# A layer's attention operands stacked with seven transfers instead of thirteen, and a new order ahead of a selective scan

## The chip, the cores and the metric

The kernel runs on one core of one Trainium2 chip. The metric is the device time of one execution, in microseconds (us). The kernel is one hand-written program: each engine (PE for matmuls, DVE, ACT, POOL, and SP, which only issues DMAs) has its own list of instructions, and semaphores order the lists against each other.

## The reference

Two layers act on x, 1024 tokens of 512 numbers. Each layer modulates a layer norm with six vectors that come from silu(c) @ wmod, and adds its two branches under gates whose magnitude is at least 0.25.

```python
ga = (2 * (ga >= 0) - 1) * jnp.maximum(jnp.abs(ga), 0.25)
h = _layernorm(x, axis=-1) * (1 + ca) + sa
x = x + ga * _L0_attn_ref(h, ...)
...
# layer 0, "attention": a selective scan
xp = jnp.einsum('bld,rd->blr', x, x_proj_w)            # 16 dt columns, 16 B, 16 C
dt = jax.nn.softplus(jnp.einsum('blr,dr->bld', dt_in, dt_proj_w) + dt_proj_b)
h = dA_t * h + dBx_t                                   # 512 channels x 16 states
y = jnp.einsum('bdn,bn->bd', h, C_t)
...
# layer 0, ffn: base linear + 8 LoRA experts under a router (softmax over 15, top 8)
...
# layer 1: 32 heads of 16, causal, linear position bias (ALiBi)
scores = jnp.einsum('bqhd,bkhd->bhqk', q, k) * SCALE + bias
out = jnp.einsum('bhqk,bkhd->bqhd', jax.nn.softmax(scores), v)
...
# layer 1, ffn: silu(gate) * up, truncated, down, truncated
```

## The kernel before

Everything stays in on-chip memory but for one round trip through DRAM, described below. Channels or tokens lie on the 128 partitions; T = 1024 tokens are two halves of 512, and 512 channels are four chunks (DC) of 128.

**Ahead of the scan.** DVE normalises the four token tiles of the first half, sums wmod weighted by silu(c) into two vectors, and PE turns them into columns (L757). PE transposes the tiles (L747), ACT applies scale and shift (L517), PE projects to dt, B and C (`x_proj`, L771; `dt_proj`, L775). ACT and DVE then work out softplus for each chunk by a longer formula: on ACT an absolute value (L542), Exp, "+1" (L545), Square, Ln (L548); on DVE the argument with the bias `dtb` (L1222) and corrections (L1234 to L1249). B and C, rows of `BCs`, are spread over the partitions by PE for each state (`broadcast`, L841 and L849). Then the second half is projected, `y_start` (L855) puts D * h into the four accumulating banks, and the scan begins.

**The scan** runs over N_ALL = 32 steps m (2 halves x 16 states), each over 4 chunks: DVE forms dBx (L1266) and scans (L1288), ACT makes the decay (L636), POOL multiplies with C (L468), PE accumulates (L889). `SLOTS` names small PE jobs that are put between steps, among them the other modulation columns (`cols`). In step 4 DVE works out the first gate in four small operations (L1293 to L1296). The ffn of layer 0 follows; its `router` (L902) takes 16 matmuls of a half after all four chunks of the transposed input.

**Queries and keys of layer 1** are 16 blocks of 128 columns x 512 tokens, in the order `QK_ORDER` (L1019, one block is four fp32 matmuls, which the trace records as eight). ACT evacuates a block to `qkf` (2 buffers), DVE splits it into three bf16 parts in `qkp` (3 buffers: block i waits until the write of block i - 3 has landed), and SP writes the parts to the DRAM array `parts_dram` [part, row, token] (L372). A row of it is a head's dimension.

**Stacks.** For each of 8 groups g of 4 heads `load_stack(g)` reads the parts back into one of three `stack` buffers: 96 partitions are six bands of 16 (a head's 16 dimensions), which hold the parts of q in the order (0,0,1,1,0,2) and those of k in the order (0,1,0,1,2,0), so that one matmul with 120 rows gives the product in full precision; 24 more rows hold the position bias (`alibi`). It takes twelve transfers of 16 partitions x 4 heads x 2 KB and one for alibi. A stack's semaphore `stk` counts all of them, and PE waits for it before the group's first scores (L963). All of these transfers and the writes are issued by SP, in one list.

**Order.** `S_QK` is the number of the QK block behind which the first early scores stand; `s_early(i)` says how many units of scores PE and DVE do behind block i. DVE's list has the split of block i, and then the maxima of those units. A unit's PSUM bank (ring of three) comes free when DVE has taken its maximum (L1403, L1407). The V projection (L1036) follows the 16 blocks, with more scores between. Stack g goes to buffer g % 3, and its load is issued when the group three before it is done with its buffer.

Of the kernel before, what the change touches and what calls it, by code (L numbers as in the profile page):

```python
# [32 lines left out]
S_QK = 8  # L33
# [9 lines left out]
PARTS_Q = (0, 0, 1, 1, 0, 2)  # L43
PARTS_K = (0, 1, 0, 1, 2, 0)
# [48 lines left out]
def program(nc, a, out):  # L93
    ctx = ExitStack()
    with ctx:
# [36 lines left out]
        dtb = tiny("dtb", [P, DC])  # L132
# [17 lines left out]
        dtw = at("dtw", G_AT + 8, [RANK, D], off=2304 + 2048 + 1024)  # L150
# [15 lines left out]
        dtin = at("dtin", 30, [RANK, HALF])  # L166
# [61 lines left out]
        for n in ("in_c in_x0 in_x1 in_wb in_w1 in_id in_misc in_l0 in_lf in_attn in_proj in_gate in_up in_down wd_p0 wd_p1 wd_p2 wd_r0 wd_r1 in_att "  # L228
                  "c_exp c_silu mod_acc mod_mm mod_ev mod_ga negA setup "
                  "ln_ve ln_rstd ln_norm ln_tr ln_hT "  # L230
                  "xp_mm xp_in bc_part bc_sub xp_bc dt_mm sp_a sp_rd sp_e sp_w sp_ln sp_z sp_u sp_w1 sp_g sp_cl sp_pu dg "
# [59 lines left out]
        for i_ in range(6):  # L291
            SLOTS[1 + i_] = ("cols", 0, 2 + i_ // 2, i_ % 2 * 2)
# [9 lines left out]
        MM_L0, MM_ALL, EV_ALL = 9, 1 + len(MODS), 2 + len(MODS)  # L302
# [10 lines left out]
        def _(sp):  # L313
# [11 lines left out]
            misc = [(sel[:].bitcast(U16), a["sel"]), (nA[:], a["A_log"]), (dtb[:], a["dt_b"]), (Dp[:], a["D"]),  # L325
# [85 lines left out]
        def _(pool):  # L411
# [7 lines left out]
            pool.memset(ones[:], 1.0).then_inc(S["setup"], 1)  # L419
            link(pool.memset(mhalf[:], -0.5))  # L420
# [77 lines left out]
        def _(act):  # L498
# [22 lines left out]
            act.wait_ge(S["in_misc"], 16 * 6)  # L521
# [16 lines left out]

            def soft(c):
                src = ps[:, 4 + c, :]  # L540
                act.wait_ge(S["dt_mm"], c + 1)
                A_(sp_log[:, c, :], src, ACT.Abs, bias=dtb[:, c:c + 1]).then_inc(S["sp_a"], 1)  # L542
                act.wait_ge(S["sp_a"], c + 1)
                link(A_(sp_exp[:, c, :], sp_log[:, c, :], ACT.Exp, scale=-1.0))
                A_(sp_w[:, c, :], sp_exp[:, c, :], ACT.Copy, bias=1.0).then_inc(S["sp_w"], 1)  # L545
# [4 lines left out]
            for part in range(3):  # L550
                bc_part(0, part)
            for c in range(DC - 1):
                soft(c)
            ln_out(0, 0, 0, 1, (1,))
            soft(DC - 1)

            def z_out(c):
                act.wait_ge(S["dt_mm"], DC + (c if c else DC))
                A_(dtT[:, c, half(1)], ps[:, c, :], ACT.Identity, bias=dtb[:, c:c + 1]).then_inc(S["sp_z"], 1)

            act.wait_ge(S["xp_mm"], 2)
            act.wait_ge(S["dt_mm"], DC)
            A_(dtin[:], ps[0:RANK, 0, :], ACT.Copy).then_inc(S["xp_in"], 1)
            bc_part(1, 0)
            z_out(1)
            bc_part(1, 1)
            z_out(2)
            bc_part(1, 2)
            act.wait_ge(S["negA"], 2)

            def prepare(i):
                c, step = i // 7, i % 7
                z, lg, e, w = dtT[:, c, half(1)], sp_log[:, c, :], sp_exp[:, c, :], sp_w[:, c, :]
                if step == 0:
                    act.wait_ge(S["sp_z"], c + 1)
# [19 lines left out]
            def slot_out(m):  # L595
# [5 lines left out]
                act.wait_ge(S["mod_mm"], 2 + MOD_NO[m])  # L601
# [20 lines left out]
            def keep_state(i):  # L622
                m, c = i // DC, i % DC
# [116 lines left out]
        def _(pe):  # L740
# [90 lines left out]
            def broadcast(m):  # L831
# [11 lines left out]
                if m:  # L843
                    pe.wait_ge(S["c_evac"], m)
# [760 lines left out]
```

## Time and profile before

| what | value |
|---|---|
| median of 3 runs | 940.39 us (939.13 to 942.77) |
| the profiled execution's own time | 939.05 us |
| its span in the trace | 937.2 us |
| PE busy | 855.5 us (91%) |
| DVE busy | 762.1 us (81%) |
| ACT busy | 439.2 us (47%) |
| POOL busy | 262.6 us (28%) |
| PE's wait for the first stack | 8.3 us |

The span is the time between the first and the last instruction in the trace; the execution's own time is 1.85 us longer. Busy shares are averages over stages with different limits, so each stage is read by itself.

### The profile page before, as it was taken

What the parts mean: (1) busy time and instruction counts of PE and PEld (TensorE: products, weight loads), DVE (VectorE), ACT (ScalarE), POOL (GpSimd) and SP (SyncE); (2) the same over time, 40 slices, a digit from 0 to 9 for tenths busy, and PEclk for the clock granted to TensorE, in tenths of its full rate; (3) what the DMA queues carried; (4) which work ended last, traced back from release to release, by engine and by line L of the source; (5) the groups of instructions that cost most, each with busy time, mean ns of one, the idle gap of its engine ahead of it and who ended that gap; (6) DMA issues with size and microseconds to landing.
All of it is one profiled execution on the core that took longest, in us unless ns stands there. A gap on an engine that the chain in (4) does not pass through costs nothing.

```text
span 937.2 us, 12092 instructions
## 1 busy us (share of the span) xinstructions
PE 855.5 (91%) x4165; PEld 410.1 (44%) x4165; DVE 762.1 (81%) x1624; ACT 439.2 (47%) x828; POOL 262.6 (28%) x213
## 2 busy tenths in 40 slices
PE   3787978899978998799999999999999999999996
PEld 2334524454427453344444444444434444444442
DVE  6589999999996876598899989998245799776776
ACT  2667655656652031100666666667541656433100
POOL 1047899999994000031000000000001334000000
PEclk8689799999999999899999999999999999999999
DMA  9200060300006006820552255310015000000001
GB/s 347 94 1 0 1 269 1 134 1 1 0 1 201 0 29 151 197 69 1 87 78 47 34 77 78 53 29 1 2 39 202 1 0 0 1 0 1 12 34 46
DMA packets 27238, 54.34 MB, mean 58 GB/s; under 512 B 5876, under 2 KB 12660, under 8 KB 25896
## 3 DMA queue, kind: packets, MB, share of 16 engines
q1 hardware_dynamic: 27176, 53.56, 21.7%
q8 instruction: 33, 0.54, 0.3%
q14 instruction: 29, 0.24, 0.1%
HBM read 44.96 MB, written 8.39 MB: 57 GB/s over the span
## 4 chain that ended last, share of the span: by engine, by line
PE 62%; DVE 6%; DMA 1%; POOL 1%; SPq 1%; ACT 1%; issue 0%; POOLq 0%
PE ps L1135 16%; PE ps L997 7%; PE ps L1146 6%; PE ps L979 6%; PE ps L1019 5%; PE ps L963 4%; PE ps L966 3%; PE ps L1056 3%; PE ps L908 3%; PE ps L1036 3%; PE ps L982 2%; DVE ps L1403 1%; PE ps L747 1%; PE ps L902 1%; DMA stack<-in_alibi 1%; PE ps L911 1%
## 5 line engine op out<-in xcount | busy, mean ns | idle before, releaser
L700 ACT ACTIVATE prob<-ps 128x512 f32<-128x512 f32 x288 | 160.1, 599 | 124.4 <-PE ps L982 96.2
L468 POOL TENSOR_TENSOR hC<-hs,C_sb 128x512 f32<-128x512 f32 x128 | 162.1, 1283 | 59.3 <-DVE hs L1288 51.3
L889 PE MATMUL ps<-hC,identf 128*128 128x512 f32 x256 | 136.1, 634 | 24.1 <-POOL hC L468 22.9
L979 PE MATMUL ps<-stack 123*128 123x512 bf16 (+3 forms) x384 | 113.8, 327 | 0.2
L636 ACT ACTIVATE ps<-dtT,nA 128x512 f32<-128x512 f32 x128 | 88.2, 689 | 47.5 <-DVE hs L1288 47.5
L424 POOL TENSOR_TENSOR rstd<-veps,mhalf 128x4 f32<-128x4 f32 x8 | 8.1, 1012 | 358.4 <-DVE veps L1173 358.4
L1410 DVE TENSOR_REDUCE mrow<-ps 128x1 f32<-128x512 f32 x128 | 82.0, 683 | 11.4 <-PE ps L966 11.2
L889 PEld LDWEIGHTS ps<-hC,identf 128*128 128x128 f32 x256 | 44.0, 194 | 90.0 <-POOL hC L468 77.3
L997 PE MATMUL ps<-prob,V 128*32 128x512 f32 (+3 forms) x768 | 81.6, 498 | 0.7 <-ACT prob L700 0.7
L1135 PE MATMUL ps<-hT,wg 128*128 128x512 f32 (+1 forms) x176 | 79.1, 592 | 0.0
L1135 PE MATMUL ps<-hT,wu 128*128 128x512 f32 (+1 forms) x176 | 79.1, 592 | 0.0
L1288 DVE TENSOR_TENSOR_SCAN hs<-ps,dBx 128x512 f32<-128x512 f32 x64 | 77.6, 1212 | 0.6 <-ACT ps L636 0.5
L1266 DVE TENSOR_TENSOR dBx<-uT,ps 128x512 f32<-128x512 f32 x112 | 73.8, 660 | 5.1 <-PE ps L841 3.9
L1403 DVE CUSTOM_DVE_ANT_0 ps<-ps,negT 128x128 f32<-128x128 f32 x256 | 66.2, 322 | 12.1 <-PE ps L963 11.3
L963 PE MATMUL ps<-stack 120*128 120x128 bf16 x640 | 62.1, 221 | 13.5 <-DMA stack<-in_alibi 8.3
L963 PEld LDWEIGHTS ps<-stack 120*128 120x128 bf16 x640 | 42.6, 98 | 62.8 <-DVE mrow L1407 13.8
L1288 DVE TENSOR_TENSOR_SCAN hs<-ps,state,dBx 128x512 f32<-128x512 f32 x56 | 69.9, 1269 | 0.2 <-ACT ps L636 0.2
L1407 DVE TENSOR_REDUCE mrow<-ps 128x4 f32<-128x512 f32 x96 | 62.5, 684 | 2.3 <-PE ps L963 1.5
L1019 PE MATMUL ps<-hT,wattn 128*128 128x512 f32 x128 | 58.2, 607 | 0.0
L1146 PE MATMUL ps<-wdp,inter 128*128 128x512 bf16 (+1 forms) x264 | 57.2, 379 | 0.0
L1135 PEld LDWEIGHTS ps<-hT,wu 128*128 128x128 f32 (+1 forms) x176 | 33.0, 188 | 42.5 <-issue 42.5
L966 PE MATMUL ps<-stack 120*128 120x512 bf16 x128 | 48.8, 383 | 2.9 <-DVE V L1388 2.1
(194 smaller groups left out, 1334.1 us busy)
## 6 DMA issues: line engine op xcount, KB each, us to landing
stack<-parts_dram SPq DMA_DIRECT2D x96, 128.0 KB
wmod<-in_wmod SPq DMA_DIRECT2D x4, 1536.0 KB, 11.3
parts_dram<-qkp SPq DMA_DIRECT2D x16, 384.0 KB, 2.7
wmod<-in_wmod SPq DMA_DIRECT2D x4, 1024.0 KB, 9.8
wattn<-in_wattn SPq DMA_DIRECT2D x1, 3072.0 KB, 10.0
wg<-in_wg SPq DMA_DIRECT2D x1, 2752.0 KB, 12.3
wu<-in_wu SPq DMA_DIRECT2D x1, 2752.0 KB, 10.5
wd<-in_wd SPq DMA_DIRECT2D x1, 2560.0 KB, 11.4
```

The lines of the kernel that those rows point to most:

```text
L468: pool.tensor_tensor(hC[:, c, :], hs[:, c, :], C_sb[:, m % 2, :], ALU.mult).then_inc(S["hc_done"], 1)
L636: A_(ps[:, DA_BANK + c % 2, :], dtT[:, c, half(h)], ACT.Exp, scale=nA[:, c * NS + s:c * NS + s + 1]).then_inc(S["da_done"], 1)
L700: A_(prob[:, u % 4, j, :], ps[:, 3 + F % 3, :], ACT.Exp).then_inc(S["exp_done"], 1)
L889: mm(ps[:, c, :], identf[:], hC[:, c, :], start=False, stop=(s == NS - 1), skip_group_check=True).then_inc(S["sum_done"], 1)
L963: ins = mm(ps[:, bank, tile(j_)], qk[0:ATT_S, 0, j_, tile(i)], qk[0:ATT_S, 1, j_, tile(kb)], start=True, stop=True)
L979: ins = mm(ps[:, bank, col:col + w], qk[0:ATT_ALL, 1, j, tile(kb)], qk[0:ATT_ALL, 0, j, q0:q0 + w], start=True, stop=not diag)
L997: ins = mm(ps[32 * j:32 * j + 32, 6 + b, q0 % HALF:q0 % HALF + w], V[:, kb, g * GH + j, :], prob[:, U % 4, j, col:col + w], start=(kb == 0 ...
L1019: ins = mm(ps[:, qk_bank(i), :], wattn[:, k, ob * P:(ob + 1) * P], hT[:, k, half(h)], start=(k == 0), stop=(k == DC - 1))
L1135: ins = mm(ps[0:M, 2 * s + b, :], w[:, k, ib * P:ib * P + M], hT[:, k, half(h)], start=(k == 0), stop=(k == DC - 1))
L1146: ins = mm(ps[:, 4 + t % 4, :], inter[0:M, k, tile(t)], wdp[0:M, part, k, :], start=(k == 0 and part == 0), stop=(k == IC - 1 and part == 2))
L1288: v.tensor_tensor_scan(hs[:, c, :], ps[:, DA_BANK + c % 2, :], dBx[:, c, :] if c < mine else dB3[m % 2], init, ALU.mult, ALU.add).then_inc ...
L1410: v.reduce_max(mrow[:, 0, j, i:i + 1], ps[:, bank, :], AX).then_inc(S["m_done"], 1)
```

## The change

**Stacks.** The host permutes the columns of w_attn and b_attn so that within a group's 64 rows the dimension runs outside and the head inside. The four heads' rows of one dimension are then contiguous in `parts_dram` (8 KB), and a band of 16 partitions takes one run per partition. Parts (0,1,2), (0,1) and (0) of q go to bands 0 to 2, 3 to 4 and 5 with one transfer each, and so do those of k, where one part is read three times, twice and once. With alibi that is seven transfers. The first stack is loaded behind write 4 instead of 5, the second behind write 6 instead of 7, and `S_QK` is 9 instead of 8.

**Ahead of the scan.** The bias of dt is a 17th row of `dtw` against a row of ones in `dtin`, so its DMA and L1222 go; the argument is read from PSUM where it is used. ACT normalises tiles 1 to 3 of the first half. "+1" moves from ACT to DVE (`plus`). The columns of the first gate (16 matmuls, one ACT copy, four DVE operations) move from the scan to a place ahead of it. `broadcast` is split into B and C, B of step 0 stands before the second projection, both of step 1 stand before `y_start`, and `y_start` is interleaved with the sums of step 0. The scan's states are kept for two chunks at a time. The router waits for each chunk of its first tile by itself.

```diff
-S_QK = 8
+S_QK = 9
...
             def load_stack(g):
-                for o, order in ((0, PARTS_Q), (1, PARTS_K)):
-                    for b, part in enumerate(order):
-                        at_ = o * D + g * GH * HD
-                        load(stack[g % 3][16 * b:16 * b + 16, o, :, :],
-                             parts_dram[part, at_:at_ + GH * HD, :].rearrange("(h d) t -> d h t", d=HD), stk[g % 3])
-                load(stack[g % 3][ATT_K:ATT_S, 1, :, :].bitcast(U16),
-                     a["alibi"][g * GH:(g + 1) * GH, :, :].rearrange("h r t -> r h t"), stk[g % 3])
+                for first, count in ((0, 3), (3, 2), (5, 1)):
+                    at_ = g * GH * HD
+                    q = parts_dram[0:count, at_:at_ + GH * HD, :].rearrange("q (d h) t -> q d (h t)", h=GH)
+                    load(stack[g % 3][16 * first:16 * (first + count), 0, :, :], q, stk[g % 3])
+                    at_, part = D + g * GH * HD, 3 - count
+                    k = parts_dram[part:part + 1, at_:at_ + GH * HD, :].rearrange("q (d h) t -> q d (h t)", h=GH)                         .to_broadcast([count, HD, GH * T])
+                    load(stack[g % 3][16 * first:16 * (first + count), 1, :, :], k, stk[g % 3])
+                load(stack[g % 3][ATT_K:ATT_S, 1, :, :].bitcast(U16), a["alibi"][g], stk[g % 3])
...
-                if i == 5:
+                if i == 4:
...
-                if i == 7:
+                if i == 6:
                     load_stack(1)
...
+            for t in range(1, 4):
+                A_(xn0[:, t, :], x_tok[:, t, :], ACT.Identity, bias=nmean[:, t:t + 1]).then_inc(S["cent"], 1)
...
+                A_(xn0[:, t, :], xn0[:, t, :], ACT.Copy, scale=rstd[:, t:t + 1]).then_inc(S["ln_norm"], 1)
...
-                A_(sp_w[:, c, :], sp_exp[:, c, :], ACT.Copy, bias=1.0).then_inc(S["sp_w"], 1)
...
+            for c in range(DC):
+                for kk in range(DC):
+                    ins = mm(ps[:, C_BANK, c:c + 1], wmod[:, kk, 2 * D + c * P:2 * D + (c + 1) * P], sc[:, 0, kk:kk + 1],
+                             start=(kk == 0), stop=(kk == DC - 1))
+            ins.then_inc(S["mod_mm"], 1)
+            broadcast_b(0)
             x_proj(1)
...
+            broadcast(1)
             pe.wait_ge(S["sp_z"], DC)
-            for c in range(DC):
-                y_start(0, c)
...
+                    if m == 0:
+                        y_start(0, c)
...
-                ts(dtT[:, c, half(0)], ps[:, 4 + c, :], dtb[:, c:c + 1], 0.0, ALU.add, ALU.max).then_inc(S["sp_rd"], 1)
...
+                ts(sp_w[:, c, :], sp_exp[:, c, :], 1.0, None, ALU.add).then_inc(S["sp_w"], 1)
...
+                stt(dt, ps[:, 4 + c, :], 0.0, lg, ALU.max, ALU.add).then_inc(S["sp_rd"], 1)
...
-                    if c == 2 and m == 4:
-                        v.wait_ge(S["mod_ev"], 4)
-                        link(ts(modt[:, 1, :], modc[:, 0, 2, :], 0.0, 2.0, ALU.is_ge, ALU.mult))
```

SP's list at the first two stacks, before (L372 writes a block's parts, L315 loads; a shape is that of the destination):

```order
L372 DMA parts_dram<-qkp 128x3x512 x6
L315 DMA stack_126<-parts_dram 16x4x1024 x12
L315 DMA stack_126<-in_alibi 24x4x1024
L372 DMA parts_dram<-qkp 128x3x512 x2
L315 DMA stack_127<-parts_dram 16x4x1024 x12
L315 DMA stack_127<-in_alibi 24x4x1024
L372 DMA parts_dram<-qkp 128x3x512 x8
```

and of the change:

```order
L371 DMA parts_dram<-qkp 128x3x512 x5
L313 DMA stack_126<-parts_dram 48x1x4096 x2
L313 DMA stack_126<-parts_dram 32x1x4096 x2
L313 DMA stack_126<-parts_dram 16x4096 x2
L313 DMA stack_126<-in_alibi 24x4096
L371 DMA parts_dram<-qkp 128x3x512 x2
L313 DMA stack_127<-parts_dram 48x1x4096 x2
L313 DMA stack_127<-parts_dram 32x1x4096 x2
L313 DMA stack_127<-parts_dram 16x4096 x2
L313 DMA stack_127<-in_alibi 24x4096
L371 DMA parts_dram<-qkp 128x3x512 x9
```

Each stack stands one write earlier, and nine writes instead of eight are behind the second.

PE's list at the first scores, before (L1019 QK blocks of four matmuls, L1025 the mask for DVE, L963 scores of stack 0):

```order
L1019 MATMUL ps<-hT,wattn 128x512 x28
L1025 MATMUL ps<-identb,negm 128x128
L963 MATMUL ps<-stack_126 128x128 x8
L1019 MATMUL ps<-hT,wattn 128x512 x4
L963 MATMUL ps<-stack_126 128x128 x4
L1019 MATMUL ps<-hT,wattn 128x512 x4
L963 MATMUL ps<-stack_126 128x128 x8
```

and of the change:

```order
L1064 MATMUL ps<-hT,wattn 128x512 x32
L1070 MATMUL ps<-identb,negm 128x128
L1008 MATMUL ps<-stack_126 128x128 x8
L1064 MATMUL ps<-hT,wattn 128x512 x4
L1008 MATMUL ps<-stack_126 128x128 x4
L1064 MATMUL ps<-hT,wattn 128x512 x4
L1008 MATMUL ps<-stack_126 128x128 x8
```

One QK block more stands ahead of the first scores; two blocks stand ahead of this piece in both.

PE's list at the start of the scan, before (L747 transposes, L771 the projection, L841 and L849 B and C, L775 and L782 the second half's dt and B/C parts, L855 `y_start`, L889 the sums):

```order
L747 MATMUL ps<-identf,xn_90 128x128 x16
L771 MATMUL ps<-hT,xpw 64x512 x4
L841 MATMUL ps<-BCs,sel 128x512
L849 MATMUL ps<-BCs,sel 128x512
...
L775 MATMUL ps<-dtin,dtw 128x512 x2
L855 MATMUL ps<-hT,dgD 128x512 x4
L841 MATMUL ps<-BCs,sel 128x512
L849 MATMUL ps<-BCs,sel 128x512
L889 MATMUL ps<-hC,identf 128x512 x4
```

and of the change:

```order
L771 MATMUL ps<-identf,xn_90 128x128 x16
L863 MATMUL ps<-sc,wmod 128x1 x16
L827 MATMUL ps<-BCs,sel 128x512
L795 MATMUL ps<-hT,xpw 64x512 x4
L840 MATMUL ps<-BCs,sel 128x512
...
L799 MATMUL ps<-dtin,dtw 128x512 x2
L827 MATMUL ps<-BCs,sel 128x512
L840 MATMUL ps<-BCs,sel 128x512
L898 MATMUL ps<-hT,dgD 128x512
L933 MATMUL ps<-hC,identf 128x512
L898 MATMUL ps<-hT,dgD 128x512
```

The gate's 16 matmuls and B of step 0 stand before the second projection, and B and C of step 1 before `y_start` instead of behind it.

## Rows read from the trace of the kernel before

**Rows 1.** The page's first line.

```profile
span 937.2 us, 12092 instructions
```

**Rows 2.** Windows: busy us (instructions) of PE, PEld, DVE, ACT, POOL; granted clock; DMA share; GB/s.

```profile
52.70:281.00 228.30, 197.08 (x649) 95.58 (x650) 222.28 (x251) 139.01 (x303) 199.91 (x160) 0.96 0.11 42
...
371.30:379.70 8.40, 0.08 (x2) 0.04 (x2) 2.44 (x5) 0.69 (x1) 0.00 (x0) 0.81 1.08 175
...
448.00:660.00 212.00, 206.19 (x1912) 99.39 (x1916) 187.70 (x659) 145.12 (x267) 0.00 (x0) 1.00 0.35 53
```

**Rows 3.** Timeline of PE around the first scores: start, length, work, [idle before, releaser].

```profile
379.66 1.04 PE L963 MATMUL ps<-stack 120*128 120x128 bf16 x8 [8.32 <-DMA stack<-in_alibi]
380.49 5.08 PE L1019 MATMUL ps<-hT,wattn 128*128 128x512 f32 x8
...
385.63 3.65 PE L1019 MATMUL ps<-hT,wattn 128*128 128x512 f32 x8
```

**Rows 4.** Timeline of SP, writes and stack loads, and the load issues of groups 2, 3.

```profile
360.68 0.36 SPq L372 DMA_DIRECT2D parts_dram<-qkp  x1
...
364.60 5.74 SPq L315 DMA_DIRECT2D stack<-parts_dram  x12
...
378.77 33.50 SPq L372 DMA_DIRECT2D parts_dram<-qkp  x8
...
448.95 6.69 SPq L315 DMA_DIRECT2D stack<-parts_dram  x12
...
477.70 6.65 SPq L315 DMA_DIRECT2D stack<-parts_dram  x12
```

**Rows 5.** The page's DMA issues: count, KB each, us to landing.

```profile
parts_dram<-qkp SPq DMA_DIRECT2D x16, 384.0 KB, 2.7
...
stack<-r SPq DMA_DIRECT2D x24, 8.0 KB, 1.9
```

**Rows 6.** DMA of the window in which stack 3 is loaded, 477.75 to 495.

```profile
DMA packets 1071, 1.81 MB, mean 105 GB/s; under 512 B 204, under 2 KB 204, under 8 KB 1068
```

**Rows 7.** Windows of 2 us: the first weights, behind PE's wait, stack 3's load.

```profile
6.00:8.00 2.00, 0.00 (x0) 0.00 (x0) 1.41 (x3) 0.00 (x0) 0.00 (x0) 1.00 1.04 422
...
380.00:382.00 2.00, 2.00 (x9) 1.27 (x8) 1.57 (x9) 0.00 (x0) 0.00 (x0) 0.50 1.11 278
...
483.00:485.00 2.00, 2.00 (x19) 1.01 (x12) 1.47 (x3) 1.29 (x4) 0.00 (x0) 1.00 1.10 134
```

**Rows 8.** DMA issues of the window 366 to 380 alone.

```profile
parts_dram<-qkp SPq DMA_DIRECT2D x3, 384.0 KB, 11.2
```

**Rows 9.** Timeline of PE: V begins, first scores of groups 2 and 3.

```profile
408.58 1.02 PE L1036 MATMUL ps<-wattn,hT 128*128 128x512 f32 x2
...
466.23 0.39 PE L963 MATMUL ps<-stack 120*128 120x128 bf16 x4
...
497.02 0.39 PE L963 MATMUL ps<-stack 120*128 120x128 bf16 x4
```

**Rows 10.** Timeline at the scan's start, all engines.

```profile
32.66 0.63 ACT L545 ACTIVATE sp_w<-sp_exp 128x512 f32<-128x512 f32 x1
33.19 0.61 ACT L546 ACTIVATE uT<-sp_exp 128x512 f32<-128x512 f32 x1
...
52.74 1.22 DVE L1288 TENSOR_TENSOR_SCAN hs<-ps,dBx 128x512 f32<-128x512 f32 x1
...
54.43 5.98 PE L855 MATMUL ps<-hT,dgD 128*128 128x512 f32 x8 [1.89 <-ACT dtT L559]
...
60.67 0.69 DVE L1266 TENSOR_TENSOR dBx<-uT,ps 128x512 f32<-128x512 f32 x1 [3.29 <-PE ps L841]
```

**Rows 11.** Timeline of DVE in step 4: the gate's four operations, first and last.

```profile
88.09 0.97 DVE L1293 TENSOR_SCALAR modt<-modc 128x4 f32<-128x4 f32 x1
...
90.52 0.16 DVE L1296 SCALAR_TENSOR_TENSOR modc<-modt 128x4 f32<-128x4 f32 x1
```

**Rows 12.** The chain that ended last, 281 to 300: the router's matmuls.

```profile
289.80 5.82 PE ps L902 x32
```

More of the change, by code:

```diff
@@ L290, in program @@
         SLOTS = {}
-        for i_ in range(6):
-            SLOTS[1 + i_] = ("cols", 0, 2 + i_ // 2, i_ % 2 * 2)
+        for i_ in range(4):
+            SLOTS[3 + i_] = ("cols", 0, 3 + i_ // 2, i_ % 2 * 2)
         for i_ in range(2):
@@ L548, in soft @@
                 A_(sp_log[:, c, :], sp_w[:, c, :], ACT.Ln).then_inc(S["sp_ln"], 1)
-            for part in range(3):
-                bc_part(0, part)
-            for c in range(DC - 1):
+            bc_part(0, 0)
+            magnitude(0)
+            bc_part(0, 1)
+            soft(0)
+            bc_part(0, 2)
+            for c in range(1, DC - 1):
+                magnitude(c)
                 soft(c)
             ln_out(0, 0, 0, 1, (1,))
+            magnitude(DC - 1)
+            act.wait_ge(S["mod_mm"], 2)
+            A_(modc[:, 0, 2, :], ps[:, C_BANK, 0:DC], ACT.Copy).then_inc(S["mod_ev"], 1)
             soft(DC - 1)
@@ L650, in _ @@
                 for c in range(DC):
-                    decay(m * DC + c)
+                    if m:
+                        decay(m * DC + c)
                     if m == 0 and c < 2:
@@ L783, in bc_rest, with slot_read, broadcast_b, broadcast_c @@
                     .then_inc(S["bc_sub"], 1)
+            def slot_read(m):
+                if m in SLOTS:
+                    if SLOTS[m][0] == "y":
+                        pe.wait_ge(S["x0"], SLOTS[m][3] + 1)
+                    else:
+                        pe.wait_ge(S["mod_ev"], 4 + MOD_NO[m])
+            def broadcast_b(m):
+                h, s = m // NS, m % NS
+                if s == 0:
+                    pe.wait_ge(S["xp_bc"], h + 1)
+                if m == 0:
+                    pe.wait_ge(S["sp_rd"], 2)
+                    pe.wait_ge(S["sp_a"], 2)
+                else:
+                    pe.wait_ge(S["dbx_done"], dbx_count(m - 1, DC - 1 if m <= NS else DC - 2))
+                    if m > NS:
+                        pe.wait_ge(S["b_evac"], m - NS)
+                mm(ps[:, B_BANK, :], sel[:, s:s + 1].to_broadcast([96, P]), BCs[:, half(h)],
+                   start=True, stop=True).then_inc(S["b_mm"], 1)
+            def broadcast_c(m):
+                h, s = m // NS, m % NS
+                if m:
+                    pe.wait_ge(S["c_evac"], m)
+                else:
+                    pe.wait_ge(S["mod_ev"], 3)
+                if m <= NS:
+                    slot_read(m - 1)
+                elif m - 2 >= NS:
+                    slot_read(m - 2)
+                mm(ps[:, C_BANK, :], sel[:, s + NS:s + NS + 1].to_broadcast([96, P]), BCs[:, half(h)],
+                   start=True, stop=True).then_inc(S["c_mm"], 1)
+            def broadcast(m):
+                broadcast_b(m)
+                broadcast_c(m)
             x_proj(0)
-            pe.wait_ge(S["in_misc"], 16 * 6)
+            pe.wait_ge(S["in_misc"], 16 * 5)
             pe.wait_ge(S["xp_in"], 1)
@@ L862, in turn @@
                         ins.then_inc(S["yt"], 1)
-            broadcast(0)
+            broadcast_c(0)
             pe.wait_ge(S["xp_in"], 2)
@@ L1555, in constants @@
     qconst = np.zeros((ATT_A, T), np.float32)
-    alibi = np.zeros((NH, ATT_A, T), np.uint16)
+    alibi = np.zeros((NG, GH, ATT_A, T), np.uint16)
     for b in range(NT):
@@ L1559, in constants @@
         for n, part in enumerate(three(sl[:, None] * (j - (b * P + 64)).astype(np.float32)[None, :])):
-            alibi[:, 3 * b + n, :] = part
+            alibi[:, :, 3 * b + n, :] = part.reshape(NG, GH, T)
     return {
@@ L1580 @@
     xpw[:, 32:64] = xp[RANK:].T
-    b_attn = g["L1_attn_b_attn"]
+    order = np.arange(2 * D).reshape(2 * NG, GH, HD).transpose(0, 2, 1).reshape(-1)
+    order = np.concatenate([order, np.arange(2 * D, 3 * D)])
+    b_attn = g["L1_attn_b_attn"][order]
     arrays = dict(
```

168 lines of the change are left out of this document (80 added, 88 removed).

## The prediction

> **What bounds the kernel now.** I read the page's span first [rows 1], then the windows by stage [rows 2]. The scan (52.7 to 281) is DVE's: 222.3 of 228.3 us busy, so time comes back there only if the scan starts earlier or DVE does less. In attention (448 to 660) PE is busy 206.2 of 212.0 us at full clock. Between them one window stands out, 371.3 to 379.7, with PE busy 0.08 us and a DMA share of 1.08. The timeline of PE [rows 3] says what it is: 8.32 us of waiting before the first scores, released by the last transfer of stack 0. SP's list [rows 4] has the twelve loads of that stack issued from 364.60, so it took 379.7 - 364.6 = 15.1 us to arrive. The reader is to see that the path runs through a load, so what matters is how long one stack's load takes and what is queued behind it, not how many instructions it has.
>
> **How fast a load is now.** During stack 3's load 134 GB/s move while the DMA engines count as fully busy, share 1.10; early in the kernel the same 16 engines move 422 GB/s [rows 7]. A stack is 12 x 128 + 192 = 1728 KB, 13 us at 134 GB/s. So busy engines here are engines held up by what they write to, 16 partitions in runs of 2 KB. The packets below 512 B tell how many engines a transfer runs on [rows 6]: thirteen transfers in that window leave 204 of them, and 204 = 12 x 16 + 12. That fits one closing packet per engine used, 16 engines for the 16-row transfers and 12 for the 24-row one. So 16 rows gave 16 engines and 24 rows 12: the largest number up to 16 that divides the outermost count.
>
> **Stacks after the change.** The new q transfer has a source of [3 parts][16][4096] against 48 destination rows, the k transfer the same with the part repeated; the next two have [2][16][4096] against 32. No row shows a transfer whose two sides differ in the outermost count. Extending what rows 6 show to both sides, the number must divide 3 and 48, so 3 engines; and 2 for the next pair. The first 16-row ones get 16, alibi 12. The price: 422 / 16 = 26.4 GB/s for an engine that nothing holds up [rows 7]. A 3-part transfer has 384 KB, 128 KB or 5.0 us on each of 3 engines; a 2-part one has 256 KB, again 128 KB or 5.0 us on each of 2. Engines 0 and 1 carry all four, 19.8 us, and about 32 KB of the rest, 1.2 us: **21.1 us**, plus 1.9 us as the smallest loads show from issue to landing [rows 5], 23.0 us per stack in place of 15. Bounds: if the destination's count decides (16 engines), runs of 8 KB over 48 partitions are no slower than now and at best 4.2 us (1728 KB at 422 GB/s). Upwards, three engines that write next to each other could be held up as today's are; at 134 GB/s for all sixteen one has 8.4 GB/s, which would give 60 us, but three together ask for only 79 GB/s, below what the row has moved, so I take the free rate.
>
> The Trainium skill says the same and speaks against the change: in "DMA: Bandwidth & Descriptors", section "Why a DMA increments its semaphore by 16 and not by 1", the number of engines is the largest up to 16 that divides the slowest count above one of both sides, and its "Rules for kernel authors" name an outermost broadcast of c copies as a confinement to c engines. Rows 6 agree for 16 and 24 rows; 3 against 48 no run here shows yet. By it the sum is the one below; without it, by the destination alone, it is the first rival's.
>
> **First stack.** Write 4 is issued at 360.68 [rows 4] and lands 2.7 us later [rows 5], so the load starts at 363.4 and ends at 363.4 + 23.0 = 386.4. PE now does one more QK block first, 3.4 us, and stands from 371.3 + 3.4 = 374.8 to 386.4: 11.6 us of wait for 8.3, though 3.4 us of it are work done earlier. After the wait PE has, before, 408.6 - 379.7 = 28.9 us to the V projection [rows 3, 9]; one block (3.65, rows 3) and one unit of scores (0.6) less, 24.7.
>
> **A second wait takes the first one's place.** SP's list is one order and today's writes already queue behind loads: in 366 to 380 they took 11.2 us instead of 2.7 [rows 8, 5]. After the change stack 1 is issued behind write 6, at about 371, and its load on engines 0 and 1 queues behind stack 0's and two writes (24 KB an engine, 0.9 us each): 386.4 + 1.8 + 21.1 = 409.3. Write 7 is issued behind it and its share on engines 0 and 1 lands at 410.3. DVE's split of block 10 reuses the buffer of write 7, so it ends at about 410.3 + 2.3; the maximum of scores unit 2 stands behind it in DVE's list (0.7 us); the bank that this frees is what PE waits for before unit 5. PE gets there at about 386.4 + 13.6 = 400.0 and goes on at 413.6: **13.6 us** more. V begins at 386.4 + 24.7 + 13.6 = 424.7, against 408.6: +16.0. Behind either wait the granted clock falls to 0.50 [rows 7]; today that costs 5.08 - 3.65 = 1.4 us on the first block and half of 1.04 on the scores, 1.9 us [rows 3]. A second wait brings a second such loss: +1.9. Together **+17.9**.
>
> **Stacks 2 to 7.** Stack 2's load is issued at 448.95 and first used at 466.23, 17.3 us; stack 3's at 477.70 and 497.02, 19.3 us [rows 4, 9]. The later four repeat this every 30.8 us. With 23.0 us stack 2 is late by 5.7, and PE has no other work in its list: +5.7, and 1.5 for the clock. Stacks 3 to 7 are late by 23.0 - 19.3 = 3.7 each, five times, +18.5; waits so short I charge no clock for. Each load is issued relative to work of the group before, so the lateness does not add up from group to group but is paid each time. Together **+25.7**.
>
> **Ahead of the scan.** ACT's chunks of softplus lose "+1", a step of 33.19 - 32.66 = 0.53 us [rows 10], four times: 2.2 us earlier at the last chunk. DVE loses four argument operations and gets four "plus", equal in number and size, and the gate's four small ones, which I charge 0.9 here. First scan -1.3. Then `y_start` (5.98 us) no longer stands before B and C of step 1, for which DVE waited 3.29 us at 60.67 [rows 10]: -3.3 there, but B and C of step 2 now come behind y_start and all four sums of step 0, 5.98 + 1.9 us of PE work, and may be late by up to 2.6. Net **-2.0**, between -0.8 and -3. The normalisation on ACT is hidden: ACT has nothing to do there, and DVE is waiting for wmod anyway. B of step 0 ahead of the second projection, the 17th row and the pairwise states cost nothing, their engines being idle or far from the bound; without this cover the 16 gate matmuls would cost some 3 us. In the scan the gate's four operations go, from 88.09 to about 90.6, 2.5 us of DVE, the bound [rows 11]: **-2.5**. The router's 16 matmuls take 5.82 us, 0.36 each [rows 12]; three of the first four can start before the last chunk is there: **-1.1**.
>
> **Sum**, against the profiled execution's own 939.05 (the median of three is 1.3 above): 939.05 - 5.6 + 17.9 + 25.7 = **977 us**. Own range of this case: 962 if the second wait is mostly absorbed, 992 if the engines run a tenth below the free rate (2.1 us more on eight loads).
>
> **Rivals.**
> 1. *The destination decides, all 16 engines work* (other sign). Then stack 0 is there in at most 15 us and likely less; it is on time if it lands by 374.8, that is within 11.4 us, 9.5 of transfer. The waits for stacks 2 to 7 are absent up to 17.3 us. For it: the transfer is issued with 48 rows of destination, and runs of 8 KB are longer. Against: nothing in the rows has such unequal sides. Time: 939.05 - 8.3 - 1.9 - 5.6 = **923**; at today's rate, landing 378.5, 928. Chance 0.14. The Trainium skill's page "SBUF — State Buffer", section "Door 1: The DMA port swizzle", has 16 partitions reach 4 of 16 ports and 48 partitions 8, which would make this case twice as fast as today; rows 7 agree as far as 134 GB/s is far under 422.
> 2. *Confined, but the second wait isn't there*, since writes do not queue behind the loads as I have it, or the steady groups have more slack than issue to use: 977 - 13.6 - 1.9 = **961**. For it: engines 3 to 15 are free for most of each write. Against: a write counts as landed only with its last engine, and 11.2 us in rows 8. Chance 0.17.
> 3. *Both effects about cancel*, a middle rate of 16 to 18 us per stack: stacks 2 to 7 in time, stack 0 landing at about 381, 6 us of wait with one more block done: 939 - 5.6 + 2 = **936 to 941**. Chance 0.04.
> 4. *The scan starts no earlier*, because DVE's list with gate and "plus" operations is the longer one there: +2 to +3 on any of these. It moves the time but not the side.
>
> **How the numbers follow.** Forecast 0.65; rival 2 0.17, rival 1 0.14, rival 3 0.04. A measurement of this kernel tells about 0.5% (4.7 us) from no change. Slower by over 0.5%: 0.65 + 0.17 + some of rival 3's, 0.83. Faster: 0.14. Within: 0.03. Range 948 to 994: it leaves out rival 1 and what lies above 994, and takes in rival 2 with a better scan start and a shorter wait. The likeliest case's own is 962 to 992.
>
> **What would show it.** Right: closing packets under 512 B in a stack's window of 3 + 3 + 2 + 2 + 16 + 16 + 12 = 54; a DMA share far below 1 during a load with some 50 to 80 GB/s; PE waits at the first scores of 11 to 12 us, in the QK stage of about 13 on DVE maxima, and of 3 to 6 us at each group's first scores, released by a stack load. V begins about 16 us later relative to the stage's start. The scan's first operation 1 to 2 us earlier, no 3.3 us wait at step 1. Wrong: no waits at first scores and a share near 1, or 16 closing packets per transfer (rival 1); a wait at stack 0 alone (rival 2). The figure that everything hangs on is the 5.0 us per engine and transfer: at 17.4 us instead of 23.0 per load the change would cost little, below 15 it gains.

## The result, and the profile of the changed kernel

The changed kernel takes 1032.75 us (median of 4, 1028.83 to 1034.25), the kernel before 940.9 us (median of 4); the ratio is 1.0975, 95% interval 1.0956 to 1.0994. It is 92 us slower, where 36 were forecast, and lies outside the range of 948 to 994. Below, the profiled execution of 1033.01 us is set against that of 939.05, a difference of 94.0.

The page of the changed kernel, its first lines and queue:

```profile
span 1031.2 us, 12042 instructions
## 1 busy us (share of the span) xinstructions
PE 884.7 (86%) x4165; PEld 423.8 (41%) x4165; DVE 760.8 (74%) x1622; ACT 439.6 (43%) x797; POOL 264.5 (26%) x214
...
q1 hardware_dynamic: 20634, 53.55, 15.3%
```

PE has the same number of instructions and 29 more busy us: it runs longer at half clock (mean granted clock 0.92 of the whole span, 0.97 before). The waits of PE from 330 to 760 (total, times, longest):

```profile
PE ps L1008 <- DMA stack<-in_alibi: 66.5, 7, 16.4
PE ps L1008 <- DVE mrow L1448: 14.4, 1, 14.4
```

Before, the first of these was one wait of 8.3 us [rows 3]; now every stack but the second is waited for. The timeline of PE through this stage and at two of the later groups, answering to rows 3 and 9 (L1008 scores, L1064 QK blocks, L1081 V):

```profile
395.58 1.03 PE L1008 MATMUL ps<-stack 120*128 120x128 bf16 x8 [16.40 <-DMA stack<-in_alibi]
396.40 5.77 PE L1064 MATMUL ps<-hT,wattn 128*128 128x512 f32 x8
...
424.19 0.61 PE L1008 MATMUL ps<-stack 120*128 120x128 bf16 x4 [14.37 <-DVE mrow L1448]
...
437.87 1.08 PE L1081 MATMUL ps<-wattn,hT 128*128 128x512 f32 x2
...
507.28 0.61 PE L1008 MATMUL ps<-stack 120*128 120x128 bf16 x4 [8.68 <-DMA stack<-in_alibi]
...
548.98 0.61 PE L1008 MATMUL ps<-stack 120*128 120x128 bf16 x4 [8.56 <-DMA stack<-in_alibi]
```

The second wait is named after a maximum of DVE. What DVE itself waited for stands in its own timeline; the row is the first instruction of the split of block 10:

```profile
420.78 0.43 DVE L1499 CAST qkp<-qkf 128x512 bf16<-128x512 f32 x1 [17.70 <-DMA parts_dram<-qkp]
```

The timeline of SP, answering to rows 4:

```profile
367.69 3.94 SPq L313 DMA_DIRECT2D stack<-parts_dram  x6
...
380.53 15.20 SPq L313 DMA_DIRECT2D stack<-parts_dram  x6
...
396.21 44.86 SPq L371 DMA_DIRECT2D parts_dram<-qkp  x9
...
520.93 3.79 SPq L313 DMA_DIRECT2D stack<-parts_dram  x6
```

From the first issue to the first scores that wait for it, stack 0 takes 395.6 - 367.7 = 27.9 us and stack 3 takes 549.0 - 520.9 = 28.1 us, in place of the 15.1 of stack 0 before. Packets of the window 521 to 550, in which one stack is loaded (rows 6), then of two stretches of it, each of them a window of its own:

```profile
DMA packets 273, 1.81 MB, mean 62 GB/s; under 512 B 54, under 2 KB 54, under 8 KB 54
...
DMA packets 93, 0.71 MB, mean 71 GB/s; under 512 B 7, under 2 KB 7, under 8 KB 7
...
DMA packets 43, 0.31 MB, mean 52 GB/s; under 512 B 5, under 2 KB 5, under 8 KB 5
```

The 54 closing packets are the 3 + 3 + 2 + 2 + 16 + 16 + 12 that the prediction named. If three engines work from 529 to 539, they move 71 GB/s, 24 each; if two work from 540 to 546, they move 52, 26 each, the free rate of 26.4.

The stages side by side; starts and ends are those of PE's first QK block, first V matmul and the end of the span:

| stage | before | after | difference | forecast |
|---|---|---|---|---|
| start to first QK block | 338.5 | 342.9 | +4.4 | -5.6 |
| first QK block to V | 70.1 | 95.0 | +24.9 | +17.9 |
| V to the end | 528.7 | 593.4 | +64.7 | +25.7 |
| sum | 937.2 | 1031.2 | +94.0 | +38.0 |

### The profile page after: what moved, and what is told of

Read it like the earlier page. It is cut to its first block, busy times and chain, and to the rows that moved or that the text cites. A ratio compares the mean times of both kernels' runs of the same rounds, so it can differ in the third digit from the quotient of the medians.

```text
span 1031.2 us, 12042 instructions
## 1 busy us (share of the span) xinstructions
PE 884.7 (86%) x4165; PEld 423.8 (41%) x4165; DVE 760.8 (74%) x1622; ACT 439.6 (43%) x797; POOL 264.5 (26%) x214
## 4 chain that ended last, share of the span: by engine, by line
PE 48%; DMA 16%; SPq 4%; DVE 2%; issue 1%; POOL 1%; ACT 1%; POOLq 0%; DVEq 0%
PE ps L1180 15%; DMA stack<-in_alibi 14%; PE ps L1191 6%; PE ps L1042 4%; PE ps L1064 4%; SPq L313 4%; PE ps L1024 3%; PE ps L1101 3%; PE ps L1008 3%; PE ps L953 3%; PE ps L1081 3%; DMA parts_dram<-qkp 2%; PE ps L771 1%; PE ps L1011 1%; PE ps L1027 1%
## 5 line engine op out<-in xcount | busy, mean ns | idle before, releaser
L468 POOL TENSOR_TENSOR hC<-hs,C_sb 128x512 f32<-128x512 f32 x128 | 162.7, 1285 | 66.5 <-ACT C_sb L662 39.6
L933 PE MATMUL ps<-hC,identf 128*128 128x512 f32 x256 | 140.1, 651 | 22.1 <-POOL hC L468 21.2
L1008 PE MATMUL ps<-stack 120*128 120x128 bf16 x640 | 67.7, 234 | 83.2 <-DMA stack<-in_alibi 66.5
L1024 PE MATMUL ps<-stack 123*128 123x512 bf16 (+3 forms) x384 | 119.4, 342 | 0.2
L1008 PEld LDWEIGHTS ps<-stack 120*128 120x128 bf16 x640 | 46.5, 104 | 139.1 <-DMA stack<-in_alibi 70.0
L1042 PE MATMUL ps<-prob,V 128*32 128x512 f32 (+3 forms) x768 | 85.2, 518 | 0.7 <-ACT prob L724 0.7
L1064 PE MATMUL ps<-hT,wattn 128*128 128x512 f32 x128 | 60.4, 627 | 0.0
```

What stands on the lines that cost most here:

```text
L468: pool.tensor_tensor(hC[:, c, :], hs[:, c, :], C_sb[:, m % 2, :], ALU.mult).then_inc(S["hc_done"], 1)
L933: mm(ps[:, c, :], identf[:], hC[:, c, :], start=False, stop=(s == NS - 1), skip_group_check=True).then_inc(S["sum_done"], 1)
L1008: ins = mm(ps[:, bank, tile(j_)], qk[0:ATT_S, 0, j_, tile(i)], qk[0:ATT_S, 1, j_, tile(kb)], start=True, stop=True)
L1024: ins = mm(ps[:, bank, col:col + w], qk[0:ATT_ALL, 1, j, tile(kb)], qk[0:ATT_ALL, 0, j, q0:q0 + w], start=True, stop=not diag)
L1042: ins = mm(ps[32 * j:32 * j + 32, 6 + b, q0 % HALF:q0 % HALF + w], V[:, kb, g * GH + j, :], prob[:, U % 4, j, col:col + w], start=(kb == 0 ...
L1064: ins = mm(ps[:, qk_bank(i), :], wattn[:, k, ob * P:(ob + 1) * P], hT[:, k, half(h)], start=(k == 0), stop=(k == DC - 1))
```

## The experiments

**The two parts alone.** First the changed kernel with the old stacks:

```diff
-                for first, count in ((0, 3), (3, 2), (5, 1)):
...
+                for o, order in ((0, PARTS_Q), (1, PARTS_K)):
```

> The changed kernel with the stacks of before (thirteen transfers of 16 partitions in 2 KB runs, behind writes 5 and 7, first scores behind QK block 8, no permuted columns): the part ahead of the scan and the router alone. If what the two traces show is the whole of it (scan ends 7.0 us later, router 2.4 us shorter), it takes 939 + 4.6, about 944 us, and PE waits 8 us for stack 0 as before. If the late scan was itself a result of something in the stacks, or of that one execution, it comes out as the prediction had it, 933 to 934 us.

Measured: 942.88 us (10 runs, 935.58 to 946.71), ratio 1.0007 (0.9981 to 1.0033). No difference to the kernel before can be measured; the expected 944 is within the spread, and none of the ten runs reaches 933. The spread is the finding: the runs of before beside them lie between 938.9 and 943.0.

Then the kernel before with the new stacks:

```diff
+                for first, count in ((0, 3), (3, 2), (5, 1)):
...
-                for o, order in ((0, PARTS_Q), (1, PARTS_K)):
```

> The kernel before with the stacks of the change alone (seven transfers, loads behind writes 4 and 6, first scores behind block 9). If the parts add up: 1033 - 4.6, about 1028 us, with loads of 28 us, waits of 16, 14 and six of 7 to 10 us. By the prediction's 23 us per load it would be 983 us.

Measured: 1029.93 us (4 runs), ratio 1.0936 (1.091 to 1.0961). The stacks are the loss, 88 of 92 us, as expected.

**Is it the engines, the run length or the rows?** The outer dimension of the source is turned:

```diff
-rearrange("q (d h) t -> q d (h t)", h=GH)
+rearrange("q (d h) t -> d q (h t)", h=GH)
...
-.to_broadcast([count, HD, GH * T])
+.to_broadcast([HD, count, GH * T])
```

> The changed kernel with the source patterns of the stacks turned: dimension outermost and part inside, [16][3][4096] and [16][2][4096], which puts partition 3d + part where part x 16 + d was, for q and k alike, so the product is the same. Same bytes, same 8 KB runs, same 48, 32 and 16 rows, same seven transfers, same places. If the outermost count of the source sets the number of engines, each transfer now uses 16 and leaves 16 closing packets, a load takes at most 15 us, no wait at the scores of stacks 1 to 7, and the kernel takes 925 to 937 us. If long runs, the 48 rows or the place of the loads are what is slow, it stays at 1020 to 1035 us.

Measured: 943.55 us (10 runs), ratio 1.0024 (0.9998 to 1.0049). 89 us come back with the same bytes, the same seven transfers, the same runs of 8 KB and the same places in SP's list. PE's waits from 330 to 760 have one stack in them:

```profile
PE ps L1008 <- DMA stack<-in_alibi: 1.8, 1, 1.8
```

That the engines have changed shows in the closing packets of a stack's window, here 486.94 to 505. They are 108, which is 6 x 16 + 12: every transfer from `parts_dram` now has 16, where the same six had 42 together.

```profile
DMA packets 327, 1.81 MB, mean 100 GB/s; under 512 B 108, under 2 KB 108, under 8 KB 108
```

The forecast of 925 to 937 for it was too low, for two reasons: the front (below), and the QK stage, which is only 2 us shorter than before although the first wait is gone. DVE still waits for a write behind the loads there:

```profile
386.15 0.43 DVE L1499 CAST qkp<-qkf 128x512 bf16<-128x512 f32 x1 [6.75 <-DMA parts_dram<-qkp]
...
398.15 0.43 DVE L1499 CAST qkp<-qkf 128x512 bf16<-128x512 f32 x1 [5.53 <-DMA parts_dram<-qkp]
```

The same with transfers of 16 rows:

```diff
+                    for b in range(count):
+                        rows = slice(16 * (first + b), 16 * (first + b) + 16)
+                        for o, part in ((0, b), (1, 3 - count)):
```

> The changed kernel with each stack loaded by twelve transfers of 16 partitions in 8 KB runs and one for alibi: the partition layout of the change, thirteen transfers. If only confinement is slow: a load of 13 to 15 us as before the change, and 930 to 940 us. If the run length of 8 KB is what slows a load, it stays far above 1000. If turned patterns (the other run) are clearly faster than this one, the reach of 48 rows matters too; if not, 16 rows are as good.

Measured: 948.01 us (4 runs), ratio 1.0072 (1.0053 to 1.0092), above the expected 930 to 940. Runs of 8 KB are not what costs the 89 us. The 16-row transfers cost a little: by the means this kernel takes 4.5 +- 2.9 us more than the turned stacks (here and below: difference of the means of all runs, and 2.1 standard errors). A load takes 16.3 us (issue 364.16, first scores 380.42), and 16-row transfers moved fewer bytes in these windows: the window 492 to 494 of this kernel and two of the turned stacks (with the old front), all with busy engines:

```profile
492.00:494.00 2.00, 2.00 (x20) 1.08 (x13) 1.47 (x3) 1.29 (x4) 0.00 (x0) 1.00 0.93 107
```

```profile
480.00:482.00 2.00, 2.00 (x22) 0.90 (x19) 2.00 (x10) 1.78 (x4) 0.00 (x0) 1.00 1.14 168
484.00:486.00 2.00, 2.00 (x25) 0.73 (x21) 1.42 (x3) 1.17 (x3) 0.00 (x0) 1.00 1.16 209
```

**Half of the confinement.** Only the 3-part transfers stay:

```diff
-                for first, count in ((0, 3), (3, 2), (5, 1)):
+                for first, count, b0 in ((0, 3, 0), (3, 1, 0), (4, 1, 1), (5, 1, 0)):
...
-                    q = parts_dram[0:count, at_:at_ + GH * HD, :].rearrange("q (d h) t -> q d (h t)", h=GH)
+                    q = parts_dram[b0:b0 + count, at_:at_ + GH * HD, :].rearrange("q (d h) t -> q d (h t)", h=GH)
...
```

> The changed kernel with only the two 3-part transfers confined; the bands of the 2-part ones are loaded by four transfers of 16 rows (nine transfers in all). The busiest engines then carry 2 x 128 KB + about 64 KB, 40 packets of 8 KB at 0.31 us, 12.4 us, instead of 68 to 72. If the busiest engine's load sets the time: a load takes 16 to 19 us, PE waits for stack 0 between the turned patterns' 1.8 and the change's 16.4 us, the second wait shrinks in step (between 2.8 and 14.4), stacks 2 to 7 are late by 2 us at most; 950 to 965 us. If any transfer with unequal outer counts costs a fixed penalty, it is still above 990.

Measured: 985.0 us (one run), between the 950 to 965 expected and the 990 of the alternative. The size in the expectation was wrong, and it is the same error as in the prediction: a load takes 26.4 us at stack 0 and 23.8 at stack 2 (issue 460.76, first scores 484.54), not 16 to 19. The busiest engines have 40 packets instead of 68, but not at 0.31 us each: while the 16-row transfers run, a packet of 8 KB takes about 1.1 us in the trace (31 packets start between 467 and 469, their median is 1.09 us). The confined engines seem to be among them: a chain of packets, each starting as the one before ends, followed back from the last packet of stack 3's load, has six in a row of 1.0 to 1.1 us there. The second wait is 6.1 us.

**Where the second wait comes from.** Stack 1 is loaded later:

```diff
-                if i == 6:
+                if i == 8:
                     load_stack(1)
```

> The changed kernel with stack 1 loaded behind write 8 instead of 6. If the second wait comes from writes queued behind a load on the confined engines, the split of block 10 no longer waits for it (write 7 lands just behind stack 0), and the wait moves to a later unit of scores, released when write 9 lands behind stack 1, some 28 us behind its issue at about 397. Time within 5 us of the change's. If the second wait has another cause (clock, ACT), it stays before the same scores unit at about the same length.

Measured: 1042.2 us (one run), 9 more than the changed kernel, where 5 at most were expected: the moved wait is 4.8 us longer, the waits for stacks are 1.9 longer in sum, and the first QK block is 1.9 later. The wait moved as expected: PE now stands 19.2 us ahead of a later unit, and DVE's row is the split of block 12, which reuses the buffer of write 9:

```profile
434.73 0.43 DVE L1499 CAST qkp<-qkf 128x512 bf16<-128x512 f32 x1 [23.11 <-DMA parts_dram<-qkp]
```

The edit moved the load, and the wait went along with it to the next write behind a load; this shows the mechanism. Its length does not follow from the load of stack 0 alone: the wait for the maximum is 14.4 us with loads of 27.9, 6.6 with 16.3 and 2.7 with the turned stacks, but 6.1 in the half-confined kernel with a load of 26.4. What counts there is when the write behind stack 1 is issued and lands, and where PE stands by then.

**Without the new front.** The turned stacks in the kernel before, everything up to the first QK block being that of before, with the first scores behind QK block 9; then the same behind block 8, which is the only edit between the two:

```diff
-S_QK = 9
+S_QK = 8
```

> The kernel before with the stacks alone, source patterns turned (dimension outermost). Front and scan as before. If the stacks' part is worth something once it is not confined: PE's 8.3 us for stack 0 shrink to about 2, and it takes 934 to 938 us, faster than both kernels. If the rest of the QK stage gives it back (DVE's maxima end last there, as in the turned run, whose stage from the first QK block to V is only 2.1 us shorter than before), it is 938 to 942.

Measured: 938.75 us (12 runs), ratio 0.998 (0.9966 to 0.9995): 0.2% faster than the kernel before. Set against the turned stacks with the new front, it also tells what the front does with the stacks out of the way: the new front is 4.1 +- 2.6 us slower by the means. With the old stacks the same difference is 0.8, within the scatter.

> As the turned stacks in front of the old prologue, but the first scores behind QK block 8 as before the change. If the extra QK block ahead of the first scores is what covers the load, PE waits 4 to 6 us for stack 0 here and the kernel takes 1 to 3 us more than with block 9. If DVE's maxima are what ends last in this stage, the two are equal within 1 us.

Measured: 939.55 us (10 runs), ratio 0.998 (0.9962 to 0.9999). PE waits 5.8 us for stack 0 instead of 2.0, and by the means it costs 0.7 +- 1.8 us: no difference. What the extra block covers comes back in waits for DVE.

**Parts of the front.** On the turned stacks with the new front (943.55; the three variants ran on another chip, on which the kernel before takes 941.3 us, for 941.5): first the gate back in the scan. The sixteen matmuls, the copy and the four DVE operations that go from the place ahead of it are left out here.

```diff
-        for i_ in range(4):
-            SLOTS[3 + i_] = ("cols", 0, 3 + i_ // 2, i_ % 2 * 2)
+        for i_ in range(6):
+            SLOTS[1 + i_] = ("cols", 0, 2 + i_ // 2, i_ % 2 * 2)
...
```

> The turned stacks with the new front (943.5 us), but layer 0's first gate again computed in the scan: six slots from step 1 on, and the four DVE operations in step 4. If the gate's 16 matmuls ahead of the second projection (6.8 us at half clock in the changed kernel's trace) are what makes the new front late, the scan starts 2 to 4 us earlier and it takes 939 to 941 us. If the clock is what decides and this part does not touch it, it stays within 1 us of 943.5.

Measured: 941.86 us (10 runs, 937.46 to 946.76), 1.7 +- 3.2 below by the means: not told apart.

Then `y_start` in one piece:

```diff
-            broadcast(1)
             pe.wait_ge(S["sp_z"], DC)
+            for c in range(DC):
+                y_start(0, c)
...
```

> The turned stacks with the new front, but with y_start for all four chunks ahead of the scan's sums and the broadcasts of step 1 behind it, as before the change. By the prediction's step this loses up to 3.3 us at step 1 and gains up to 2.6 at step 2: about 944. If the interleaving is what costs (step 1 and step 2 both wait for B in the changed kernel, 2.9 and 2.8 us), it takes 939 to 941 us.

Measured: 943.16 us (10 runs, 940.12 to 950.40), 0.8 +- 3.4 above: not told apart either. Its trace has one wait of DVE for B of 8.9 us, in place of the two of 2.9 us at steps 1 and 2 with `y_start` interleaved.

**PE kept busy at the start**, in both fronts:

```diff
+            pe.wait_ge(S["setup"], 1)
+            for _ in range(44):
+                mm(ps[:, 3, 0:P], ones[:], ones[:], start=True, stop=True)
             pe.wait_ge(S["in_id"], 16)
```

> The turned stacks with the new front, and 44 fp32 matmuls of 128x128 on a matrix of ones, into a bank that nobody reads before it is overwritten, ahead of the first transposes, where PE has nothing to do for 11 us. They are work added, not computation changed. If half-clock stretches ahead of and in the scan are what the new front loses by, and they follow from what PE did before, these stretches move or shrink and the time falls by 3 to 8 us. If only the amount of work matters, nothing changes (943 to 944).

Measured: 939.37 us (10 runs, 935.57 to 946.72), 2.9 +- 3.8 below: a hint, not shown.

> The same 44 matmuls in the kernel with the old front and the turned stacks (938.75 us). The old front has 27 us of half clock up to 60 us, the new one some 37. By the theory of the clock this one gains less than the new front, 1 to 4 us; if the two gain the same, the clock is no difference between the fronts.

Measured: 939.87 us (10 runs), 0.6 +- 1.7 above the 938.75 without them: nothing.

**Bands apart.** What was still open is the size of a load.

```diff
-                for first, count in ((0, 3), (3, 2), (5, 1)):
+                for first, count in ((3, 3), (0, 2), (2, 1)):
```

> The changed kernel with the bands of a stack in another order on the partitions: the 3-part transfers fill partitions 48 to 95 instead of 0 to 47, the 2-part ones 0 to 31, the single ones 32 to 47. Same transfers, same engines, same bytes. In the changed kernel 8 KB packets take 0.31 us alone, but some of 0.6 us appear only while three engines write partitions 0 to 15, 16 to 31 and 32 to 47. If two bands 32 partitions apart share a way in, as the Trainium skill's port table has it, the packets of that phase now take 0.31 us, a load takes 25 to 26 us instead of 28.1, and the kernel 1005 to 1022 us. If the longer packets come from the DRAM side (two engines reading the same part for k), nothing changes: 28 us, 1028 to 1035.

Measured: 1020.48 us (2 runs), ratio 1.0852 (1.082 to 1.0883), within the expected 1005 to 1022, though a load is longer than the expected 25 to 26 us. Packets of a window in which three engines load stack 3, here 521 to 531:

```profile
DMA packets 100, 0.75 MB, mean 75 GB/s; under 512 B 9, under 2 KB 9, under 8 KB 9
```

They move 75 GB/s instead of 71. Of the packets of 8 KB, 10 of 84 took twice 0.31 us in the changed kernel's window 529 to 539, here 2 of 89. A load takes 27.1 us instead of 28.1, all seven waits 58.7 us instead of 66.5. So the place of the bands matters, as loads into partitions 0 to 15 and 32 to 47 at once would have it. In the Trainium skill, "SBUF — State Buffer", section "Door 1: The DMA port swizzle", partitions 32 apart are on the same port; this trace agrees. But that is 1 us of the missing 5. Of the 12 us of time another 4.6 are the front's scatter (first QK block at 338.3 instead of 342.9).

## Why the prediction was right in direction and wrong in size

**Confinement to 3 and 2 engines: right.** The closing packets are 54, as named; the turned patterns leave 108 and take the 89 us back. The rule of the Trainium skill ("DMA: Bandwidth & Descriptors", section "Why a DMA increments its semaphore by 16 and not by 1") agrees with the traces, now also where the two sides' counts differ: 3 against 48, 2 against 32, and 16 against 48 and 32.

Of the 56 us between the forecast of +38.0 and the measured +94.0, some 31 are the length of a load (4.8 at the first stack, 25.9 at the six later ones), 13 are the clock behind the later waits, 10 are ahead of the QK blocks, and 2 the rest of the QK stage.

**The 23.0 us per load: wrong, 28.** This is the term that failed, in the step "21.1 us, plus 1.9". It takes each packet of the busiest engines at the free rate. Two engines alone do keep it (26 GB/s each), but in the first part of a load the 16-row transfers and alibi run on all engines at once with the confined ones; there packets take about 0.5 to 1.2 us instead of 0.31, which the half-confined kernel shows in its 23.8 us. In the changed kernel the same kind of chain, followed back through stack 3's load, has 69 packets of 8 KB in 26.0 us, where 69 at 0.307 us are 21.2. Some 3.4 us of the excess fall before 529, 1.2 of them in the very first packet, and 1.4 between 529 and 537, where packets of 0.6 us stand among those of 0.31; of these about 1 us goes away with the bands apart. Which engine a packet ran on is not in the trace, so this split is an estimate.

**The first stack.** Forecast 11.6 us of wait, measured 16.4: the 4.9 us of the load. The second wait: forecast 13.6, measured 14.4. Its chain (write 7, split of block 10, maximum, bank) was right, but its times were not, and that the length agrees is partly luck. The prediction had SP issue stack 1 at about 371 and write 7 right behind it; SP took until 396.2 to get to write 7, which landed when DVE went on at 420.8, 10 us later than the forecast 410.3. PE also came to the wait 10 us later, at 409.8 instead of 400.0, so the two errors cancel. With what the clock costs behind both, +24.9 for +17.9.

**Stacks 2 to 7: the largest miss,** +64.7 for +25.7. The six waits are 66.5 - 16.4 = 50.1 us, where 24.2 were forecast: 28.1 against a window of 19.3 is 8.8 per group instead of 3.7. The other 14.6 us are the clock, which I had charged to stack 2 alone (1.5): from V to the end PE is busy for 526.5 us instead of 510.1 over as many matmuls. With each wait comes a stretch at 0.50. The windows of one group, first scores to first scores, before, in the changed kernel and in the half-confined one:

```profile
466.23:497.02 30.79, 29.93 (x282) 14.57 (x281) 28.15 (x102) 20.80 (x38) 0.00 (x0) 1.00 0.42 60
```

```profile
507.28:548.98 41.70, 32.75 (x281) 15.91 (x281) 28.54 (x101) 21.04 (x38) 0.00 (x0) 0.87 0.16 44
```

```profile
484.54:519.67 35.13, 31.62 (x282) 15.43 (x282) 28.52 (x101) 21.07 (x38) 0.00 (x0) 0.94 0.27 52
```

A group takes 41.7 us for 30.8: 8.6 of wait and 2.3 of slower matmuls. "Waits so short I charge no clock for" was an assumption without a row, and wrong even for the 3.7 us that were forecast: in the half-confined kernel PE waits 3.1 to 4.5 us per group, and its matmuls still take 31.6 us instead of 29.9.

**Ahead of the scan: -5.6 forecast, +4.4 measured.** The router's part was too small: its chain has 3.45 us for 5.82 [rows 12], 2.4 instead of 1.1. The rest failed at PE. The first scan is at 54.05, not 51.4. The wait at step 1 was to go and is still there: steps 1 and 2 both wait for B (2.9 and 2.7 us), and in the half-confined kernel, whose front ran faster, they do too (2.9 and 2.4). In the changed kernel later steps wait as well, in the half-confined one none of them up to 170. DVE's waits for B from 62 to 170, before and in the changed kernel (one of 3.3 us stands ahead of the first window):

```profile
DVE dBx L1266 <- PE ps L841: 0.6, 1, 0.6
```

```profile
DVE dBx L1318 <- PE ps L827: 10.0, 6, 2.9
```

The wait at 61.62 counts in the second. I had hidden the gate's 16 matmuls behind other work at "some 3 us"; they take 6.8 in the changed kernel, and the 3.03 us that eight matmuls for the earlier columns take in the trace of before would have said 6. What they take depends on the clock. Two executions with the same instructions up to here, the changed kernel at 0.50 and the half-confined one at 0.74 over these matmuls:

```profile
37.69 6.83 PE L863 MATMUL ps<-sc,wmod 128*128 128x1 f32 x32
```

```profile
35.56 4.87 PE L863 MATMUL ps<-sc,wmod 128*128 128x1 f32 x32 [0.52 <-DVE dtT L1294]
```

Seven profiled kernels share the new front to the letter, four the old one; granted clock of the window 0 to 334 and the start of the first QK block:

| front | clock | first QK block at |
|---|---|---|
| new, turned stacks | 0.89 | 346.9 |
| new, stack 1 late | 0.90 | 344.8 |
| new, the change | 0.91 | 342.9 |
| new, old stacks | 0.91 | 340.7 |
| new, 16-row transfers | 0.92 | 339.3 |
| new, bands apart | 0.92 | 338.3 |
| new, 3-part only | 0.95 | 334.5 |
| old, before | 0.93 | 338.5 |
| old, with the change's stacks | 0.95 | 339.9 |
| old, turned stacks, block 9 | 0.95 | 338.2 |
| old, turned stacks, block 8 | 0.95 | 338.7 |

At 0.95 the new front, in its one execution there, is some 4 us ahead of the old, near the forecast, though partly by the larger gain at the router; at 0.91 it is behind. Its time follows the clock over 12 us, that of the old front lies within 2. This fits how the runs of one kernel come to spread from 935.6 to 946.7. The runs' own clocks say the same: of the ten runs of the new front with the old stacks, the four with a mean clock of 0.957 or 0.958 take 943.9 to 946.7 us and the three with 0.974 to 0.979 take 935.6 to 939.3. That half clock is the cause is read from identical instruction lists at different clocks; no experiment set the clock by itself. Which part of the front lowers it more often is open: taking the gate or `y_start` back, or keeping PE busy at the start, told nothing beyond the scatter.

**The rivals.** The destination doesn't decide (rival 1): with the destination unchanged, the turned source alone gives 16 engines. The second wait was there (rival 2); the loads were slower than assumed, not of a middle rate (rival 3). Rival 4, a scan that starts no earlier, held, but through PE, not through DVE's list.

## What to carry to other kernels

Merging DMAs is a change of the access pattern's outermost count first: look at the closing packets and at GB/s over DMA share, and put a dimension of 16 outermost on the side that has a small count there (here two letters that change places in a rearrange, and the counts of a broadcast with them, worth 89 us). Size a confined load by a row in which the same mixture of transfers runs, not by the free rate. Charge the clock with a wait of PE that comes back in every group (here 2.3 us a group with waits of 8.6, and still 1.7 us of PE with waits of 3 to 4.5). Where PE sets the start of a stage at half clock, a faster order can be an unstable one, so compare many runs.

## What was not expected

- SP is held up by what it issues: the six transfers of stack 1 took 15.2 us to issue in the changed kernel, for 3.9 at stack 0 and 3.6 with the turned patterns, and the last of them went out when stack 0 had landed. So all writes behind them were issued late too, not only queued.
- With all 16 engines on 16 rows, runs of 8 KB moved 107 GB/s in a window, and the turned stacks, with transfers of 48, 32 and 16 rows, 168 to 209; they are loaded in some 13 us.
- Over identical instructions the granted clock up to the first QK block differed between executions from 0.89 to 0.95, 12 us of this kernel's time.
